# A 32-tile ring for the gather passes of a four-layer graph network on Trainium2

## What is computed

```python
x = x + L0(relu(layernorm(x)))   # attention: softmax weights per destination
x = x + L1(relu(layernorm(x)))   # sum of edge_weight * (h @ W)[src]
x = x + L2(relu(layernorm(x)))   # three mean convolutions, 128 -> 256 -> 256 -> 128
x = x + L3(relu(layernorm(x)))   # three relational convolutions, 8 edge types
# the core of L0 and of each convolution of L3:
out = segment_sum(table[row_of(src, edge_type)] * weight[:, None], dst, num_segments=5000)
```

## Time and profile before

| | us |
|---|---|
| median of 3 runs | 6639.18 |
| lowest, highest | 6638.15, 6643.88 |
| span of the profiled execution | 6637.1 |
| pass 0, first to last gather | 322.7 to 1281.7 |
| pass 5 | 3818.7 to 4742.4 |
| pass 6 | 4788.4 to 5702.7 |
| pass 7 | 5730.0 to 6626.5 |

### The profile page before, as it was taken

How to read it: one execution, slowest core, us unless ns; L and a number is a source line. 1 busy time by engine, 2 the same in 40 slices (tenths; PEclk the granted TensorE clock), 3 DMA queues, 4 the chain that set the end, 5 groups by cost and what they waited for, 6 DMA issues and landing times.

```text
span 6637.1 us, 91610 instructions
## 1 busy us (share of the span) xinstructions
PE 4400.9 (66%) x24058; PEld 3411.2 (51%) x24058; DVE 2758.0 (42%) x8998; ACT 1117.3 (17%) x2098; POOL 4090.1 (62%) x3645
## 2 busy tenths in 40 slices
PE   3466666666666662999989977777766666533333
PEld 1344445544444442988876755555555555433333
DVE  7965656577777775322236511111111111111111
ACT  2522222122222221111113401111100000000000
POOL 2346666478888883753445466666466666566666
PEclk5566666666666665999999978878867777655555
DMA  5722222255555655754457744444333333211111
GB/s 158 229 90 78 77 78 76 73 99 99 99 100 99 103 99 159 225 159 125 127 165 249 263 127 132 132 133 133 124 104 112 112 115 112 77 50 51 52 52 49
DMA packets 589026, 779.12 MB, mean 117 GB/s; under 512 B 87945, under 2 KB 484000, under 8 KB 578000
## 3 DMA queue, kind: packets, MB, share of 16 engines
q1 hardware_dynamic: 347276, 437.26, 20.7%
q0 software_dynamic: 190256, 287.00, 19.3%
q10 hardware_dynamic: 51334, 52.94, 2.4%
HBM read 533.39 MB, written 243.79 MB: 117 GB/s over the span
## 4 chain that ended last, share of the span: by engine, by line
PE 35%; issue 16%; another core or an unknown queue 16%; DVE 12%; POOL 10%; DMA 5%; DVEq 3%; ACT 1%; POOLq 0%; ACTq 0%; SPq 0%
PE PS L2408 10%; PE PS L2284 6%; POOL ring L915 6%; PE PS L2321 5%; POOL part L934 4%; DMA part<-ring,cur 4%; PE PS L2250 3%; DVE ACC_B L1699 2%; PE PS L2545 2%; PE PS L2311 2%; PE PS L2346 1%; DVE ACC_B L1697 1%; DVE QSEL L1720 1%; PE PS L2286 1%
## 5 line engine op out<-in xcount | busy, mean ns | idle before, releaser
L2284 PE MATMUL PS<-QSEL,ring 128*128 128x64 f32 x7436 | 1362.4, 334 | 762.8 <-issue 350.3
L2284 PEld LDWEIGHTS PS<-QSEL,ring 128*128 128x128 f32 x7436 | 1319.4, 251 | 973.4 <-issue 793.0
L934 POOL DMA_INDIRECT part<-ring,cur x625 | 1005.9, 1609 | 244.5 <-issue 175.8
L915 POOL DMA_INDIRECT ring<-tab_l3b,SRC x625 | 599.1, 959 | 361.3 <-issue 223.5
L915 POOL DMA_INDIRECT ring<-tab_l,SRC x593 | 586.8, 990 | 373.4 <-issue 164.0
L915 POOL DMA_INDIRECT ring<-tab_l3a,SRC x625 | 596.2, 954 | 353.1 <-issue 201.1
L915 POOL DMA_INDIRECT ring<-tab_l3c,SRC x625 | 596.2, 954 | 327.4 <-issue 210.3
L2250 PE MATMUL PS<-ACC_B 128*128 128x320 f16 x2568 | 619.0, 408 | 194.7 <-DVE ACC_B L1699 101.7
L1733 DVE TENSOR_TENSOR ACC_B<-ACC_B,PS 128x128 f32 (+1 forms) x314 | 79.7, 254 | 1400.4 <-remote 998.4
L2321 PE MATMUL PS<-XM,SCR 128*128 128x512 f32 x960 | 571.0, 727 | 40.2 <-issue 36.8
L2346 PE MATMUL PS<-SCR,SEL 128*32 128x128 f32 x1250 | 277.5, 404 | 406.7 <-DVE SCR L1774 355.6
(11 more groups left out here) (486 smaller groups left out, 6901.4 us busy)
## 6 DMA issues: line engine op xcount, KB each, us to landing
ring<-pairs_d SPq DMA_DIRECT2D x60, 1280.0 KB
pairs_d<-ACC_B ACTq DMA_DIRECT2D x320, 160.0 KB
SCR<-pairs_d SPq DMA_DIRECT2D x40, 1280.0 KB
tab_l3a<-SCR SPq DMA_DIRECT2D x40, 1024.0 KB, 4.3
tab_l3b<-SCR SPq DMA_DIRECT2D x40, 1024.0 KB
SCR<-in_src SPq DMA_DIRECT2D x125, 320.0 KB
ACC_A<-pairs_d SPq DMA_DIRECT2D x20, 1280.0 KB
tab_l3c<-SCR SPq DMA_DIRECT2D x40, 512.0 KB
```

The lines of the kernel that those rows point to most:

```text
L915: pool.indirect_dma_start(ring[:, slot, 0:width], None, tab[p][:, :], bass.IndirectOffsetOnAxis(SRC[:, t:t + 1], 0)).then_inc(sem(f"pair_i ...
L934: pool.indirect_dma_start(part_d[j][:, :], bass.IndirectOffsetOnAxis(cur[:, s:s + 1], 0), ring[:, s, 0:D], None, compute_op=ALU.add).then_ ...
L2284: ins = mm(PS[:, s, ch * QWIN:(ch + 1) * QWIN], rows, hot, start=e == 0 and ch == 0, stop=e == end, skip_group_check=True)
```

## The change

The ring becomes 32 slots deep. Where rows are 128 wide (passes 0 and 7) all 32 slots lie in the old ring buffer, slot s at columns 128 s. Where they are 256 wide (passes 5 and 6), slots 0 to 15 are where they were and slots 16 to 31 lie in the first 4096 columns of MULTI. The eight landing semaphores are now quad_in0 to quad_in7, each for four slots, and PE waits once a quad for all four tiles of it. POOL's wait for mm_done now asks for the quad eight quads back. PE's first two turns, a loop before in passes 5 to 7, are written out, and a turn's slots are the lower or the upper half by its parity.

```diff
-SLOTS = 2 * BUNCH
+SLOTS = 2 * TURN
+        far_ring = MULTI[:, 0:BUNCH * 2 * HID].rearrange("p (s f) -> p s f", f=HID)
+        def gathered(p, slot):
+            if PASS[p]["F"] == D:
+                return ring_flat[:, slot * D:(slot + 1) * D]
+            return ring[:, slot, :] if slot < TURN else far_ring[:, slot - TURN, :]
+        def landings(quad, first=0):
+            return sum(t % SLOTS // QUAD == quad for t in range(first, T))
-                        pool.indirect_dma_start(ring[:, slot, 0:width], None, tab[p][:, :],
-                                                bass.IndirectOffsetOnAxis(SRC[:, t:t + 1], 0)).then_inc(sem(f"pair_in{slot // 2}"), 16)
+                        pool.indirect_dma_start(gathered(p, slot), None, tab[p][:, :],
+                                                bass.IndirectOffsetOnAxis(SRC[:, t:t + 1], 0)).then_inc(sem(f"quad_in{slot // QUAD}"), 16)
-                        if e % 2 == 0 and ahead is None:
-                            pe.wait_ge(sem(f"pair_in{slot // 2}"), landed)
+                        if e == 0 and ahead is None:
+                            pe.wait_ge(sem(f"quad_in{slot // QUAD}"), landed)
-                            rows = ring[:, slot, ch * P:(ch + 1) * P] if ahead is None else X[:, ahead * P:(ahead + 1) * P]
+                            rows = gathered(p, slot)[:, ch * P:(ch + 1) * P] if ahead is None else X[:, ahead * P:(ahead + 1) * P]
+                        half, filled = (i % 2, 0) if b is None else (u, r + 1)
+                            slot = half * TURN + j
-                    turns(pe, turn, apart=p == 0)
+                    turns(pe, turn, apart=True)
```

More of the change, by code:

```diff
@@ L2266, in sums, with landed @@
                     pe.sem_inc(sem("turn"), 1)
-                    def landed(j, i):
-                        per, first = 32 * TURNS + 16 * (j < 2), 32 * (TURNS - LAG) + 16 * (j < 2)
+                    def landed(slot, i):
+                        per, first = 16 * landings(slot // QUAD), 16 * landings(slot // QUAD, LAG * TURN)
                         earlier = k * first if p == 0 else km * first + pe.snap(km * (ORD[p] - 1) + k) * per
-                        return earlier + i * 32 + 32
+                        return earlier + (i + 1) * (16 * QUAD)
                     def tile(g, s, e, slot, landed, end, ahead=None):
-                        if e % 2 == 0 and ahead is None:
-                            pe.wait_ge(sem(f"pair_in{slot // 2}"), landed)
+                        if e == 0 and ahead is None:
+                            pe.wait_ge(sem(f"quad_in{slot // QUAD}"), landed)
                         if ahead == 0:
@@ L2291, in turn @@
                         added = pe.snap(kq + TURN // QUAD * i + CREDIT)
+                        half, filled = (i % 2, 0) if b is None else (u, r + 1)
                         for j in range(TURN):
[L2293 removed]
+                            slot = half * TURN + j
+                            tile(4 * i + j // QUAD, j // QUAD, j % QUAD, slot, None if p == 0 and b is None else landed(slot, filled if p else r), QUAD - 1,
                                  TURN * i + j if p == 0 and b is None else None)
@@ L2299, in turn @@
                                 span(pe.snap(k * EARLY + PER_TURN * i + x), SPAN_SLOT[x])
-                    turns(pe, turn, apart=p == 0)
-                    tile(QUADS - 1, 0, 0, 0, landed(0, TURNS - LAG if p == 0 else TURNS) - 16, 0)
+                    turns(pe, turn, apart=True)
+                    last = (T - 1) % SLOTS
+                    tile(QUADS - 1, 0, 0, last, landed(last, T // SLOTS - (LAG * TURN // SLOTS if p == 0 else 0)) - 16 * (QUAD - 1), 0)
                     added = pe.snap(kq + QUADS + CREDIT)
```

2 lines of the change are left out of this document (removed).

## The result

| | before | changed |
|---|---|---|
| median of 7 runs each, us | 6639.18 | 6661.15 |
| lowest, highest | 6635.2, 6643.91 | 6656.6, 6670.74 |
| span of the profiled execution | 6637.1 | 6659.5 |
| ratio, 95% interval | | 1.0035 (1.0025 to 1.0045) |

Forecast were 38 us fewer (6601.0 us); 22 us more were measured. The time is inside the range (6480 to 6690), the sign is wrong. In what follows the chip of these runs is called the first chip, for the kernel before takes 6639 us on it alone: on the five chips of the experiments it takes 6103 to 6113 us. The changed kernel itself ran on three of these five.

A forecast was written before the change was run, and what follows sets the result against it. The four gather passes were taken as bound by POOL's 1.25 us a gather plus 579 us of stops waiting for late quads. Terms -8 + 0 + 0 - 30 = -38 us gave 6601 us, range 6480 to 6690.

The forecast's parts named there:

- What bounds: Four gather passes: 1.25 us a gather plus 579 us of POOL stops; POOL's silence releases PE's late increments.
- adds that come late without any stop of POOL after them: Sign in the changed profile, named beforehand, that would show the prediction wrong; no size given.
- Pass 0, -8 us: Start of pass 0: 16 more gathers run before PE starts; -8 us, bounds 0 and -20.
- Passes 5 and 6, the cycle, 0: Steady state: four quads released a cycle, which stays 23.5 us; depth is a phase, not a rate; 0 us.
- Passes 5 and 6, both ends, 0: Start loses 0 to 20 us, end gives back 7; each pass between -7 and +13 us, booked 0.
- less what PE can still do: Start of passes 5 and 6: PE's four PSUM banks reduce the loss of 0 to 20 us; no size given.
- Pass 7, -30 us: Pass 7: PE catches up between stops, so POOL runs longer before stopping; 30 us freed, bounds 0 and 100.
- a phase and nothing else: Rival, chance 0.20: pass 7 behaves as pass 6, only pass 0's 8 us are gained; 6631 us.
- The landing wait for four tiles and the place of the second half, 0: PE's one landing wait a quad and other addresses in MULTI: covered by the ring or harmless, booked at 0.
- Slower: longer stands: Rival, chance 0.20: PE stands longer at starts of passes 5, 6, 7, up to 20 us each; up to +52 us.
- POOL would run 20 us longer: Start of passes 5 and 6: POOL issues 20 us longer than today's 29.7 us while PE holds quads back.
- The rule weighed: Skill's rule: increments about 26 ns after a matmul's end; by it nothing is held and the absorption rival would be the forecast.

The follow-up runs named there:

- The pair made by hand: Changed kernel, passes 5 to 7, every fourth quad's VectorE add waiting for memsets at POOL's stop: POOL 16 tiles ahead 6342.21 us, 32 tiles 6357.93 us.
- with 16 tiles too: Changed kernel with POOL's wait brought back to 16 tiles everywhere: 1.0011, 1.0008, 1.0006 and 1.0003 of the kernel before, on four chips.
- the kernel with 32 tiles: Changed kernel, passes 5 to 7, every fourth quad's add waiting for memsets at POOL's stop, POOL waiting for the quad 32 tiles back: 6357.93 us, 1.0418.

## Why the prediction was wrong, point by point

**Where the miss came from.** From -38 us forecast to +22 us measured is 60 us. Pass 7 made 32.9 of it (+2.9 for -30), the ends of passes 5 and 6 made 25.6 (+15.9 and +9.7 for 0), pass 0 with its later start made 10.4 (+2.4 for -8), and the rest, booked at nothing, took 8.5 off. Two steps failed: that a deeper ring buys running time in pass 7, and that the loss at a pass's start is softened and returned at its end.

**What bounds.** That the passes are 1.25 us a gather plus stops is right, and the other chips show it plainly: without stops passes 5 to 7 take 788 to 801 us. That POOL's silence ends the lateness fits the start of each pass at both depths (in pass 6 the third add is 14.1 us late with 16 tiles and 35.6 us with 32, each time behind POOL's stop) and nearly all of pass 6. It doesn't fit pass 7, where 23 late adds before and 40 in the changed kernel came while POOL was issuing. The prediction named "adds that come late without any stop of POOL after them" as a sign of being wrong. Its reading of pass 7 rests on one quad and two stops, and the even stops that it argued from are those of pass 6 (3.1 to 4.4 us, but for one): in the kernel before, pass 5's range from 1.1 to 4.5 us and pass 7's from 1.2 to 5.7 us. What holds the increments stays open, since no chip that holds came up again.

**Pass 0, -8 us: wrong in size, the bound of 0 was right.** The first stop fell from 49.03 to 33.05 us, much as said (29). The pass took 1.1 us more. POOL was through 19.4 us sooner and the end grew by 20.6 us: DVE and PE set this pass, not POOL.

**Passes 5 and 6, the cycle, 0: right.** Idle times of 327.4 and 315.2 us against "near 328 and 316". Depth is a phase there, most plainly in pass 6.

**Passes 5 and 6, both ends, 0: wrong, and what turned the sign.** The sum had a loss of 0 to 20 us at the start, netted against 7 us of gain at the end, bounds -7 to +13. Measured +15.9 and +9.7. The start costs the whole 20 us (the fifth quad comes 19 to 24 us later, and quad 148 still 20 to 22), not a part of it. PE's four PSUM banks, which I took to soften it, soften nothing that can be seen in these times. The gain at the end was 4 and 12 us, near the 7 booked. So the step that failed is "less what PE can still do".

**Pass 7, -30 us: wrong.** The step was "here PE catches up with POOL between the stops, so a deeper ring does buy running time". It bought none: POOL's idle time fell by 8 us, and the stops became fewer and longer, 26 with 110.5 us where there were 35 with 121.7 (gaps over 0.9 us), 4.25 us each in place of 3.48. The lateness of the adds grew instead, 9.7 us in the mean against 6.0. This is what the rival "a phase and nothing else" said in words ("a burst after a long stand brings as many of them as it saves"). The start cost some 20 us here too, and a PE that is 293 us busy in 904 gave back 19 at the end: +2.9 us. The pair made by hand has -4.0. Why the longer run bought nothing isn't shown. The step took increments to be held until a stop, and many came through while POOL ran, up to 24.2 us late.

**The landing wait for four tiles and the place of the second half, 0: right** where nothing is held: 1.0003, 1.0005 and 1.0003. On the first chip no run separates them from the depth.

**The rivals.** "Slower: longer stands" was the one: the place (starts of passes 5 to 7), the point from which it decides (PE, not POOL, sets the pass: most in pass 5, least in 7) and the sign are as it said; its price of up to 20 us a pass came out as 15.9, 9.7 and 2.9. I gave it 0.20, because I put each end's unknown in the middle of its bounds. A loss of 20 us had a row (POOL would run 20 us longer), its softening had none; the sum should have gone by the row.

**The rule weighed.** The Trainium skill's "TensorE: Matmul & The Clock Gate", section "The cost: per-tile semaphore tail", puts an increment at about 26 ns behind a matmul. In passes 5 to 7 of the kernel before and the changed one, with 16 tiles too, on four other chips an add follows 0.23 us in the mean behind the recorded end of its quad, so there nothing speaks against it. On the first chip it is 3.8 to 6.0 us in the mean in the kernel before, up to 9.7 us in the changed one, and 35.6 us at the worst place shown above. The trace doesn't agree there, unless the recorded ends of matmuls are wrong by as much.

## What to carry to other kernels

Before a ring is made deeper, ask what ends the lateness that it is to cover. Lateness that ends by itself is absorbed (130 us here); lateness that the producer's own pause ends is put off by the added depth at the start, and the consumer, further behind at the end, returns it only where it has room. The second half is shown by the kernels with stands made by hand, 13 us in passes 5 to 7 of one profiled run of each; for the first chip it is the best reading of passes 5 and 6 and not shown by a run there. And one late event beside one stop doesn't tell what ended it: count the late events that have no stop beside them. And read a pass as two numbers, the producer's run and the consumer's tail behind it: a gain in the first that stands again in the second is no gain.

## What the runs showed of the hardware

**Chips differ by 8% on this kernel.** Before takes 6639 us on one chip and 6103 to 6113 us on five, with nearly the same mean granted clock of the changed kernel (0.72 against 0.73 to 0.74). Whether it is the chip or something around it the runs don't tell. The difference is made in the four gather passes. Nor is it PE alone that is slower there: in passes 5 to 7 of the kernel before, 64 of SP's 148 DMA instructions take over 0.45 us, up to 1.38 us; on the second chip none of 148 takes over 0.38 us.

**On the first chip PE crawls in places while POOL issues indirect DMAs.** The lone matmuls in the timeline above start 2.1 and 2.8 us apart, multiples of 0.70 us, and such steps lie between many matmuls of pass 6: from start to start, within 0.03 us of 0.70, 1.40, 2.10 or 2.80 us, the kernel before has 193 with 252 us in all, the changed one 206 with 279 us; on the second chip the kernel before has 18, with 14 us. In pass 5 there are 75, 95 and 13. In the kernel before, in its fifth quad of pass 6, lone matmuls start at 4817.52, 4818.92 and 4820.32, 1.40 us apart.

It would fit late increments and late matmuls in pass 6 that one queue of PE's is served once in 0.70 us while POOL issues, and empties when POOL stops. That is only argued, and pass 7 of the changed kernel speaks against it as a whole: there the adds are latest, not one such step stands, and the 26 matmuls shown above start 0.21 us apart beside a running POOL. No run took it apart, since no other chip showed it.

**POOL's sequencer runs some 12 gathers ahead of the engine.** An increment of its own came 15 us before the place where it stands in the text. Where the signal hung on a memset of the engine, the add came only with it, 50.8 to 51.1 us behind the first gather in the kernel with 32 tiles.

**A wait for POOL's own memset costs 0.84 to 0.95 us between gathers**, most of it in the wait and the restart: five memsets take 0.25 us of it.
